# First conditions as four small runs, a weight chunk converted by two engines, and weights on a second DMA queue

## What is computed

```python
W = cond_weights[condition]                  # (64, 32, 32), one of 16 matrices for each batch
y = einsum('bct,bcd->bdt', x, W)             # x: (64, 32, 512) -> y: 64*32 rows of 512
base = y @ W_base.T + b_base                 # 512 -> 512
probs = softmax(y @ W_gate.T)                # 8 experts; the two best, weights made to sum to 1
h = einsum('bnd,erd->bner', y, A)            # 8 experts x 16 ranks
delta = einsum('bner,eor->bno', h * route_w[..., None], B)
out = x + base + delta
```

## Time and profile before

| | us |
|---|---|
| median of 3 runs | 95.22 |
| lowest and highest | 95.0, 95.29 |
| the profiled execution, its own time | 95.87 |
| span of its instructions | 94.0 |
| PE busy, share of the span | 90.2, 96% |
| DVE busy | 65.3, 69% |
| ACT busy | 23.5, 25% |
| HBM read and written | 6.35 MB, 4.19 MB |

### The profile page before, as it was taken

How to read it: one execution, slowest core, us unless ns; L and a number is a source line. 1 busy time by engine, 2 the same in 40 slices (tenths; PEclk the granted TensorE clock), 3 DMA queues, 4 the chain that set the end, 5 groups by cost and what they waited for, 6 DMA issues and landing times.

```text
span 94.0 us, 1811 instructions
## 1 busy us (share of the span) xinstructions
PE 90.2 (96%) x643; PEld 86.6 (92%) x643; DVE 65.3 (69%) x228; ACT 23.5 (25%) x55; POOL 16.2 (17%) x29
## 2 busy tenths in 40 slices
PE   6998999999999999999999999999999999999980
PEld 2397899999999999999999999999999999999970
DVE  2884997867575866867575866777575968867660
ACT  4065813311304031311304031311304031311210
POOL 5158404120404040120404040120400000000000
PEclk9999999999999999999999999999999999999999
DMA  1999163340607042330507061330606020302023
GB/s 38 292 319 369 59 192 142 112 121 34 196 0 222 8 163 74 124 106 36 194 0 224 13 192 38 125 108 37 194 9 222 1 112 0 112 7 112 0 112 112
DMA packets 6360, 10.65 MB, mean 113 GB/s; under 512 B 1008, under 2 KB 1616, under 8 KB 6352
## 3 DMA queue, kind: packets, MB, share of 16 engines
q1 hardware_dynamic: 5616, 10.12, 33.0%
q0 software_dynamic: 448, 0.23, 1.0%
q10 hardware_dynamic: 288, 0.20, 0.7%
HBM read 6.35 MB, written 4.19 MB: 112 GB/s over the span
## 4 chain that ended last, share of the span: by engine, by line
PE 87%; DMA 6%; SPq 2%; DVE 1%; ACT 1%; issue 0%
PE main_ps L521 53%; PE y_ps L508 13%; PE main_ps L537 11%; DMA w_raw<-w_all 6%; PE main_ps L597 5%; PE main_ps L603 3%; PE hwT_ps L531 2%; SPq L208 1%; DVE x_sb L489 1%; ACT w_hi L281 1%; SPq L211 0%; SPq L213 0%; PE main_ps L636 0%
## 5 line engine op out<-in xcount | busy, mean ns | idle before, releaser
L521 PE MATMUL main_ps<-w_hi,y_hi 128*128 128x320 f32 x112 | 27.1, 322 | 0.4 <-ACT w_hi L281 0.4
L521 PE MATMUL main_ps<-w_lo,y_hi 128*128 128x320 f32 x112 | 26.9, 321 | 0.0
L521 PE MATMUL main_ps<-w_hi,y_lo 128*128 128x320 f32 x112 | 25.8, 312 | 0.0
L258 POOL DMA_INDIRECT mixw<-cond_w,row_ids x14 | 14.0, 1002 | 48.7 <-PE y_ps L508 46.2
L521 PEld LDWEIGHTS main_ps<-w_hi,y_lo 128*128 128x128 f32 x112 | 19.0, 188 | 0.0
L521 PEld LDWEIGHTS main_ps<-w_hi,y_hi 128*128 128x128 f32 x112 | 18.0, 190 | 0.9 <-ACT w_hi L281 0.9
L521 PEld LDWEIGHTS main_ps<-w_lo,y_hi 128*128 128x128 f32 x112 | 18.5, 189 | 0.1
L508 PE MATMUL y_ps<-mix,x_sb 128*128 128x128 f32 x124 | 16.9, 279 | 0.0
L508 PEld LDWEIGHTS y_ps<-mix,x_sb 128*128 128x128 f32 x124 | 16.0, 195 | 0.1
L291 ACT ACTIVATE second<-top 128x1 f32<-128x1 f32 x16 | 4.7, 296 | 42.7 <-DVE top L389 42.7
L427 DVE TENSOR_TENSOR x_sb<-main_ps,x_sb 128x512 f32<-128x512 f32 x15 | 10.3, 690 | 4.8 <-PE main_ps L537 4.7
(11 more groups left out here) (66 smaller groups left out, 87.0 us busy)
## 6 DMA issues: line engine op xcount, KB each, us to landing
x_sb<-x SPq DMA_DIRECT2D x16, 256.0 KB, 3.1
out<-x_sb SPq DMA_DIRECT2D x15, 256.0 KB, 2.1
w_raw<-w_all SPq DMA_DIRECT2D x4, 324.0 KB, 5.6
b_raw<-b_lora SPq DMA_DIRECT2D x1, 256.0 KB, 6.3
bias_sb<-bias SPq DMA_DIRECT2D x1, 256.0 KB, 4.4
mixw<-cond_w,row_ids POOLq DMA_INDIRECT x14, 2.7
out<-x_sb ACTq DMA_DIRECT2D x1, 128.0 KB, 1.8
out<-x_sb SPq DMA_DIRECT2D x1, 128.0 KB, 1.8
```

The costliest lines, as they stand in the source:

```text
L258: pool.indirect_dma_start(mixw[:, t, :], None, cond_w, bass.IndirectOffsetOnAxis(row_ids[:, t:t + 1], 0))\
L521: last = pe.matmul(main_ps[t % 2][:, half, 0:n_cols], y, w[:, half * HALF:half * HALF + n_cols], start=i == 0, stop=i == STEPS - 1)
```

## The change

1. The conditions of tiles 0 and 1 are loaded on their own: a DMA of four runs of 8 bytes (`first_cond`, one partition). DVE turns it into one row (`first_row`, 1 x 8) and PE spreads that row with ones of one partition. `first_channel` and its two GpSimd instructions are gone, and so is a wait. The full `cond` is loaded by ACT, and DVE waits for it at `row_ids`.
2. ACT issues, behind the table: cond and the four weight chunks. SP issues the four runs, x of tiles 0 and 1, waits until weight chunk 1 has landed, and then issues b and x of tile 2.
3. Of chunk 1 (`SHARED_CHUNK`), ACT converts columns 0 to 319 and DVE columns 320 to 647, which PE waits for as well.
4. The first warm-up is 3 of 512 columns and one of 256 in place of 5 of 512.

```diff
-    WARM_BEFORE, WARM_BEHIND, WARM_BETWEEN, WARM_AFTER = (512,) * 5, (512, 512), (128,), ((512,), (128,))
+    WARM_BEFORE, WARM_BEHIND, WARM_BETWEEN, WARM_AFTER = (512, 512, 512, 256), (512, 512), (128,), ((512,), (128,))
+    first_conds = cond.rearrange("(q c) t -> c q t", c=C)[0:1, :, 0:PICKED]
...
-            sp.dma_start(cond_sb[:, :], cond).then_inc(cond_landed, 16)
+            sp.dma_start(first_cond[:, :, :], first_conds).then_inc(first_cond_landed, 16)
             load_x(0)
-            load_w(0)
             load_x(1)
-            load_w(1)
-            load_w(2)
-            load_w(3)
+
+            sp.wait_ge(w_landed[1], 16)
             sp.dma_start(b_raw[:, :], b_lora).then_inc(b_landed, 16)
             load_x(2)
...
-            pool.memset(first_channel[:, :], 0.0).then_inc(cleared, 1)
-            pool.wait_ge(cleared, 1)
-            pool.affine_select(out=first_channel[:, :], in_=first_channel[:, :], compare_op=ALU.not_equal,
-                               fill=float(C), base=0, pattern=[[-C, Q]], channel_multiplier=1)\
-                .then_inc(first_channel_ready, 1)
...
-                act.activation(w_hi[:, c, :], w_raw[:, c, :], ACT.Copy).then_inc(w_hi_ready, 1)
+                n = slice(0, HALF if c == SHARED_CHUNK else ALL)
+                act.activation(w_hi[:, c, n], w_raw[:, c, n], ACT.Copy).then_inc(w_hi_ready, 1)
...
             act.dma_start(table[:, 0, :, :], cond_w.rearrange("(p k) d -> p k d", k=K)).then_inc(table_landed, 16)
+            act.dma_start(cond_sb[:, :], cond).then_inc(cond_landed, 16)
+            for c in range(CHUNKS):
+                act.dma_start(w_raw[:, c, :], w_chunks[c, :, :]).then_inc(w_landed[c], 16)
             split_w(0)
...
-            dve.wait_ge(cond_landed, 16)
-            dve.wait_ge(first_channel_ready, 1)
-            dve.tensor_tensor(own_cond[:, :, :], first_channel[:, :].unsqueeze(1).to_broadcast([P, PICKED, Q]),
-                              cond_sb[:, 0:PICKED].unsqueeze(2).to_broadcast([P, PICKED, Q]),
-                              ALU.mult).then_inc(own_cond_ready, 1)
+            dve.wait_ge(first_cond_landed, 16)
+            dve.tensor_scalar(first_row[:, :, :], first_cond[:, :, :].rearrange("p q t -> p t q"), float(C), None,
+                              ALU.mult).then_inc(first_row_ready, 1)
...
+            def high_w_rest():
+                dve.wait_ge(w_landed[SHARED_CHUNK], 16)
+                dve.tensor_copy(w_hi[:, SHARED_CHUNK, HALF:ALL], w_raw[:, SHARED_CHUNK, HALF:ALL])\
+                    .then_inc(w_rest_ready, 1)
+                dve.wait_ge(w_rest_ready, 1)
...
             select(0)
+            dve.wait_ge(cond_landed, 16)
...
+            high_w_rest()
             low_w(1)
             low_w(2)
             low_w(3)
...
-            pe.wait_ge(own_cond_ready, 1)
-            pe.matmul(cond_ps, ones[:, 0:P], own_cond[:, :, :], start=True, stop=True).then_inc(cond_spread, 1)
+            pe.wait_ge(first_row_ready, 1)
+            pe.matmul(cond_ps, ones[0:1, 0:P], first_row[:, :, :], start=True, stop=True).then_inc(cond_spread, 1)
...
                 if n == 0:
                     pe.wait_ge(w_hi_ready, c + 1)
+                    if c == SHARED_CHUNK:
+                        pe.wait_ge(w_rest_ready, 1)
```

More of the change, by code:

```diff
@@ L52, in adaln_ffn_kernel @@
     FIRST_ORDER = [(0, 0), (0, 1), (0, 2), (1, 0), (1, 2), (2, 0), (1, 1), (2, 2), (2, 1), (3, 0), (3, 2), (3, 1)]
+    SHARED_CHUNK = 1
     STEPS = len(ORDER)
@@ L97, in adaln_ffn_kernel @@
         expert_ids = sb("expert_ids", [P, E])
-        first_channel = sb("first_channel", [P, Q])
-        own_cond = sb("own_cond", [P, PICKED, Q], bf16)
+        first_cond = sb("first_cond", [1, Q, PICKED], i32)
+        first_row = sb("first_row", [1, PICKED, Q], bf16)
         PARTS = 3
@@ L137, in adaln_ffn_kernel @@
         mixw_landed = [sem(f"mixw_landed{t}") for t in range(PICKED, TILES)]
+        first_cond_landed = sem("first_cond_landed")
         cond_landed = sem("cond_landed")
@@ L142, in adaln_ffn_kernel @@
         bias_landed = sem("bias_landed")
-        first_channel_ready = sem("first_channel_ready")
         row_less_channel_ready = sem("row_less_channel_ready")
@@ L151, in adaln_ffn_kernel @@
         ident_ready = sem("ident_ready")
-        own_cond_ready = sem("own_cond_ready")
+        first_row_ready = sem("first_row_ready")
         cond_spread = sem("cond_spread")
@@ L160, in adaln_ffn_kernel @@
         w_hi_ready = sem("w_hi_ready")
+        w_rest_ready = sem("w_rest_ready")
         w_lo_ready = sem("w_lo_ready")
@@ L208, in load_x @@
                 sp.dma_start(x_sb[:, t, :], x_tiles[t, :, :]).then_inc(x_landed[t], 16)
-            def load_w(c):
-                sp.dma_start(w_raw[:, c, :], w_chunks[c, :, :]).then_inc(w_landed[c], 16)
-            sp.dma_start(cond_sb[:, :], cond).then_inc(cond_landed, 16)
+            sp.dma_start(first_cond[:, :, :], first_conds).then_inc(first_cond_landed, 16)
             load_x(0)
-            load_w(0)
             load_x(1)
-            load_w(1)
-            load_w(2)
-            load_w(3)
+            sp.wait_ge(w_landed[1], 16)
             sp.dma_start(b_raw[:, :], b_lora).then_inc(b_landed, 16)
@@ L239, in _ @@
         def _(pool):
-            pool.memset(first_channel[:, :], 0.0).then_inc(cleared, 1)
-            pool.wait_ge(cleared, 1)
-            pool.affine_select(out=first_channel[:, :], in_=first_channel[:, :], compare_op=ALU.not_equal,
-                               fill=float(C), base=0, pattern=[[-C, Q]], channel_multiplier=1)\
-                .then_inc(first_channel_ready, 1)
             pool.iota(row_less_channel[:, :, :], [[1, K], [-1, C]], base=0, channel_multiplier=K,
                       allow_small_or_imprecise_dtypes=True).then_inc(row_less_channel_ready, 1)
-            pool.wait_ge(first_channel_ready, 1)
             pool.wait_ge(row_less_channel_ready, 1)
@@ L265, in _ @@
             pool.memset(ident[:, :], 0.0).then_inc(cleared, 1)
-            pool.wait_ge(cleared, 2)
+            pool.wait_ge(cleared, 1)
             pool.affine_select(out=ident[:, :], in_=ident[:, :], compare_op=ALU.not_equal, fill=1.0,
```

## The result

The changed kernel takes 95.61 us (median of 22 runs, 95.34 to 96.41), the kernel before 95.30 us (22 runs beside them). The ratio is 1.0038, with a 95% interval from 1.0020 to 1.0057: by the ratio 0.36 us slower (the medians differ by 0.31), where 0.30 us faster was forecast. Its profiled execution took 95.86 us with a span of 94.1 us, the same as the one shown of before (95.87 and 94.0). So these two traces cannot explain the difference by themselves.

A forecast was written before the change was run, and what follows sets the result against it. PE's start at (2,0) was taken as the bound, set by chunk 2's landing. Chunk 2 landing 0.30 us earlier, other parts at 0, gave a median of 95.22 - 0.30 = 94.92, said as 94.9 us; range 94.35 to 95.4.

The forecast's parts named there:

- The bound: At the start, PE's last wait is for w_hi at (2,0), 9.65 us, chunk 2's landing plus 0.79 us.
- The landings: Weights on ACT's queue: chunks 1, 2 and 3 each land 0.3 us earlier, bounds 0 and 1.2 us.
- 1.2 us over pace: Chunk 1 lands 2.07 us behind x of tile 1, read as slow packets that a second queue could pass.
- rival 1: First loads: landings do not move and the second gap swallows the split; 95.2 us, chance 0.27.
- The split: Chunk 1's conversion: ACT's half 0.44 us, DVE's 0.50, w_hi complete 0.24 us earlier; alone it brings 0.
- DVE is free then: When chunk 1 lands, DVE can convert its half at once, having waited 1.24 us before 8.77.
- Behind (2,0): PE's steps after (2,0): no new wait for b, x of tile 2 or the last w_lo; otherwise the forecast is wrong.
- The four small runs: First conditions: landing in 1.2 to 1.7 us, taken as 1.4; mix weights up to 0.2 us earlier, value 0.
- x later: x of tile 1, sharing with weights, lands at about 6.4 us for 5.92, costing PE 0 to 0.1 us.
- The five issues ahead of ACT's table load: ACT's issues at the start take 2.3 us, covered by 2.78 us of idle time before its first conversion.
- Rival 3: PE's start: the shorter warm-up makes the clock rise later; mean loss 0.8 us, 96.0 us, chance 0.11.
- Four fifths: Share of the forecast's own case, weighted 0.45, taken to lie beyond the 0.29 us a measurement can tell.

The follow-up runs named there:

- the first two looks: First and second profiled executions of the unchanged kernel before: 95.87 and 94.89 us.
- e6: Kernel before with only the split added, chunk 1 converted by ACT and DVE: 95.50 us, ratio 0.9987.
- e13: Kernel before with two DVE memsets between the landing of the conditions and the row, no DMA moved: 95.32 us, ratio 0.9991.
- e7: Kernel before with only b and the third x held back until chunk 1 has landed, all loads on SP's queue: 95.25 us, ratio 0.9983.
- e18: Kernel before with only b and the third x held back until chunk 1 has landed, run a second time: 95.34 us, ratio 1.0000.
- the three looks: Three profiled executions of the changed kernel: 95.86, 95.94 and 95.87 us.
- e1: Changed kernel with the first conditions and warm-up of before; weights on ACT's queue and split stay: 95.43 us, ratio 1.0007 to the kernel before.
- e2: Changed kernel with the long first warm-up of before, 5 matmuls of 512 columns: 95.56 us, ratio 1.0021 to the kernel before.
- e5: Kernel before with the DMA part alone, weight chunks on ACT's queue, b and third x held back until chunk 1 has landed: 95.52 us, ratio 1.0008.
- e11: Kernel before with x of tile 1 ahead of chunk 0, b and third x held back, chunk 1 converted by both engines: 95.74 us, ratio 1.0058.
- e3: Kernel before with the first conditions as four small runs alone, full table of conditions on ACT's queue: 95.60 us, ratio 1.0034.
- e4: Kernel before with the shorter warm-up alone, 3 of 512 columns and one of 256: 95.35 us, ratio 0.9991.
- e9: Kernel before with the conditions issued by ACT ahead of the other table, SP beginning with x of tile 0: 98.05 us, ratio 1.0265.
- e8: Kernel before with one more, unused DMA of four runs of 8 bytes on SP behind the conditions: 95.84 us, ratio 1.0039.
- e17: Kernel before with five DVE memsets between the landing of the conditions and the row, no load moved: 95.42 us, ratio 1.0022.

## Why the prediction was wrong, point by point

- **The bound.** For the trace shown it was read rightly: PE's last wait on the way, (2,0) at chunk 2's landing plus 0.79. But the trace was one execution of a start that varies by 1 us. I had written that it lay 0.65 us above the median and then took its waits as those of the median.
- **The landings, the step that failed first.** The gain of 0.30 us was counted from chunk 1 at 7.99 and chunk 2 at 8.86. In the changed kernel ACT's starts on chunks 1 to 3 were 7.67, 8.35 and 9.16, for the 7.7, 8.6 and 9.4 forecast. But 7.99 is the latest of six one-queue traces in which ACT waited for chunk 1 (7.99, 7.07, 7.59, 7.57, 7.09, 7.55: the first two looks, e6, e13, e7, e18). With the weights on ACT's queue SP, which waits for chunk 1, went on at 7.52, 7.91, 7.50, 7.37, 7.37 and 6.71 (the three looks, e1, e2, e5), though ACT had issued it some 0.4 to 0.9 us earlier. The two groups lie in the same place, 7.5 and 7.4 in the mean, and e5 gives 1.0008. In the second look at before chunk 1 landed 1.3 us behind x of tile 1 and not 2.1, so that most of the "1.2 us over pace" was that one execution's. The term of 0.3 us for packets of x that pass in a stall is borne out by no run, and rival 1 (landings do not move, 95.2) was right for this part. The Trainium skill's rule (DMA: Bandwidth & Descriptors, Issuing engines are not separate DMA queues), which the prediction cited, agrees with that number.
- **Chunk 0, the term that was missing.** I worked out that x of tile 1 would come later by sharing, and not that chunk 0 shares as well. It came at 6.16, 6.47 and 6.14 for 5.25, 4.96 and 5.10 (4.89 to 5.63 in the nine traces with the loads issued as before), about 1.1 us later; e1 and e2 have 6.07 and 5.76, but e5, with the queues of e1, 5.24. The Trainium skill (DMA: Bandwidth & Descriptors, Queues, rings and completion order) says that a DMA engine takes turns between the queues for which it has work. The late chunk 0 agrees; in one queue it had stood ahead of x of tile 1.
- **The split.** ACT's half: 0.46 us for the 0.44 forecast. DVE's copy of 328 columns: 0.39 us, in the second look 0.32, for the 0.50 that I took from the two-operand rows. Nearer was the estimate of 0.33 worked out from the Trainium skill (VectorE: DVE Perf Modes, on the two-port mode): the 0.32 and the 0.33 of e6 agree with it, the 0.39 lies a fifth above. "DVE is free then" failed in all three traces: with chunk 0 late, its w_lo and two y_lo stood ahead, and DVE's half began 0.68, 0.74 and 0.82 us behind ACT's. PE waited 0.15 and 0.26 us for it in two of three.
- **Behind (2,0), the sign of being wrong that came.** I had checked the last w_lo, due at (3,1), with 0.1 us to spare, and not that of chunk 2, due at (2,1): by my own sum it was ready at 10.20 and due at 10.25. PE waited there 0.11 and 0.19 us in the second and third look, and in e1, e2 and e11, all of them kernels with the split.
- **The four small runs, the step with the wrong sign.** "Four runs cannot take longer" than 128: they landed 2.04 us after the issue's start (0.74 to 2.78) for 1.7, outside my bounds of 1.2 to 1.7, of which the 1.2 had no row behind it. DVE made the row at 2.62 to 2.81 in the five traces with them (the three looks, e2, e3), and at 2.41 to 2.57 in all traces with the whole table issued first by SP and no memset ahead of the row. And I had no term for the issue: SP was held 0.74 us for 0.38, and x with it. I had put this part at 0. Alone it costs 0.34% (e3), in the changed kernel 0.13 us by one pair (e2 and e1), so it is the best supported cause of the loss, and how much of the 0.36 us it explains stays open.
- **x later.** Forecast 6.4 for tile 1. PE waited for it until 7.17 and 6.79 in two looks, so 0.4 to 0.8 us later than forecast, and once 0.96 us for x of tile 0, for which I had no term. That this comes of the sharing is not shown: e6 and e13 waited for it until 6.83 and 6.86 with all loads in one queue.
- **What held.** The five issues ahead of ACT's table load: it ended at 5.03, chunk 0 came at 6.16. b landed 2.7 us after its issue, at 10.2, and neither b nor x of tile 2 was waited for. From the turn on nothing changed within 0.12 us in 20 traces.
- **Rival 3 (the clock).** The first trace looks like it, with 0.77 us more for the mixes. Two more looks had the rise by the first mix, so it is not in every execution; that the shorter warm-up makes a late rise more frequent is neither shown nor refuted (e4).
- **The range** of 94.35 to 95.4 had no case for a start in which x and the row come later at the same time; 95.61 lies above it. "Four fifths" of my forecast beyond 0.29 us was too much for a value of 0.30.

## What to carry to other kernels

Where one execution's profile lies well above the median, look at a second and a third before a wait in it is priced, and look at their times too: here the first trace lay above the median and the next two below. At the start of this kernel, where everything waits for first loads, the waits moved by up to 1 us from one execution to the next. Traces of experiments that leave a stage alone are further looks at that stage. A load of fewer bytes or fewer runs need not be cheap: count the issue time on its engine, what is queued behind it, and what large load is in flight beside it. The second queue changed no time here (1.0008); list every load that will share, also the one that comes next, and ask which engine's cover goes when that one is late. And when work is moved to an engine that is "free then", follow what stands behind it on that engine to every step that needs it, not only to the last.

## What the runs showed of the hardware that I had not expected

- A DMA of four runs of 8 bytes, from four rows of `cond` in DRAM into one partition, held SP for 0.72 to 0.74 us in six traces, one of 128 runs of 64 bytes for 0.38. It landed 2.04 us after the issue's start in the first trace, against 1.7.
- Loads of 8 and 64 KB, issued beside the first 256 KB load and not ahead of it, landed 1.06 and 1.96 us later (e9; the second was issued 0.44 us later): the largest effect of any edit here, 2.65%.
- A delay of 0.78 us on SP ahead of all x and weights cost 0.37 us of time (e8). One of 0.5 us on the first row cost 0.2 us, with an interval that holds zero (e17).
- ACT waited for the same chunk, issued at the same instant in the same kernel, until 7.99 us in one execution and 7.07 in another; in a third it was free at 7.14, and the chunk was there.
